# First attention of a two-attention kernel: score products made twice with full 128-row operands instead of once with transposed weights

## The chip, the cores and the metric

The kernel runs on one core of one Trainium2 chip. The metric is the device time of a launch in microseconds (us). Every engine of the core (TensorE, VectorE, ScalarE, GpSimd) runs its own instruction stream; in the profile they are PE, DVE, ACT and POOL, and SyncE, which only issues DMAs, is SP. Semaphores order the streams. TensorE reads SBUF and writes PSUM (8 banks of 128 x 512 floats); VectorE and ScalarE read and write both; GpSimd is used on SBUF alone here.

## What is computed

The reference is a chain of six blocks on x of shape (8, 512, 128): gated feed-forward, attention, gated feed-forward, expert feed-forward, a second kind of attention, expert feed-forward. The change is in the first attention alone (16 heads of 8 dimensions, 8 sequences of 512 tokens, a band of at most 60 tokens to either side):

```python
q = (x @ Wq + bq).reshape(B, S, H, hd).transpose(0, 2, 1, 3)
k = (x @ Wk + bk).reshape(B, S, H, hd).transpose(0, 2, 1, 3)
v = (x @ Wv + bv).reshape(B, S, H, hd).transpose(0, 2, 1, 3)
scores = jnp.einsum('bhqd,bhkd->bhqk', q, k) * inv_sqrt
band = jnp.abs(idx[:, None] - idx[None, :]) <= half
scores = jnp.where(band[None, None], scores, -1e+30)
attn = jax.nn.softmax(scores, axis=-1)
out = jnp.einsum('bhqk,bhkd->bhqd', attn, v)
out = jnp.einsum('bhqd,hdk->bhqk', out, W_o)
return out.transpose(0, 2, 1, 3).reshape(B, S, D) @ Wfc + bfc
```

## The kernel before

The kernel is a row of phases with a barrier between them: a start (P), a feed-forward (F0a), the first attention (A0), and then F0b, F1a, A1, F1b. In A0 (`attn0`, lines 956 to 1374) the 8 sequences are 8 chunks, one iteration each of a loop that each engine runs in its own code; the order on an engine is the written order, and the counting semaphores named below tie the engines together.

A chunk has 4 query tiles of 128 tokens. Because of the band a tile needs only a window of 256 keys (192 at both ends of the sequence). A unit `n` (16 in a chunk) is one query tile `t = n // 4` and four heads. To keep float precision in a cheap product, q and k are split in a rounded part and a rest (`fp32r` is the rounded type), so a head has 24 rows: q-high, q-high, q-low against k-high, k-low, k-high. Head rows are padded to 32, so four heads fill 128 partitions.

Per unit before:
- PE `scores` (L1254): four products, one per head, each with 24 rows in its own quarter of the array, queries on the output's partitions.
- DVE (L1203, `tensor_tensor_reduce`): one instruction per head adds the mask and takes the maximum, `M` goes to SBUF and the maximum to `nmax`.
- ACT (L1088): one Exp per head with the maximum as its bias.
- PE `turn` (L1266): 8 transposes of the weights, so that keys are on the partitions.
- ACT (L1011, first key block) and DVE (L1013, second key block), `copy_turned`: PSUM to `PT` in SBUF (`PT` lies over `dn1`, so its name in the trace is dn).
- PE `outputs` (L1279), for two units at once: values against weights, 16 products.

At the end of a chunk PE projects q, k and v of the next (`project`, L1298 and L1304), DVE adds the biases and builds the split rows (`rows_vector`, L1158 to L1179), and then PE turns Q and K (L1314), ACT copies Q (L1071) and DVE copies K (L1188) before the next scores can start. GpSimd only adds a bias to the values (L1040) and takes a reciprocal root for a layer norm (L155). The layer norm of an older chunk (L130 to L177) and the output of the last chunk (L673 to L704) run between the units.

The phase ends with `turn_out`, divide, `turn_back`, `project_out` of the last chunk and two layer norms, one after the other.

## Time and profile before

| | |
|---|---|
| median of 3 runs | 3268.33 us (3264.53 to 3269.55) |
| the profiled execution's own time | 3267.73 us |
| its span, first to last instruction | 3265.8 us |
| PE busy | 2641.5 us, 81% |
| DVE busy | 2432.7 us, 74% |
| ACT busy | 2312.6 us, 71% |
| POOL busy | 1636.1 us, 50% |
| mean granted TensorE clock | 0.849 |

Busy time is an average over all phases. What A0 is worth is read from its own stretch: its first instruction is POOL's at 426.93 us and the next phase's first work is at 943.92 us. "Granted clock" is the share of TensorE's full speed that it was given. A matmul's end is modelled, so a matmul of 0.39 us can be followed by the next one after 0.23 us: durations of PE are read together with the distance between starts.

### The profile page before, as it was taken

To read this page: it belongs to the slowest core of one execution; us is meant where nothing else is said; L and a number is where in the kernel's file an instruction comes from. 1 tells how busy PE (TensorE), PEld (TensorE's weight loads), DVE (VectorE), ACT (ScalarE), POOL (GpSimd) and SP (SyncE) were. 2 spreads that over 40 slices of the span, in tenths; PEclk is the share of its full clock that TensorE was granted. 3 is DMA by queue.
4 is the path that set the end of the run, shared out by engine and by line. 5 is a ranking of instruction groups with operands and counts; after the bars stand their busy time and mean duration, and the time that the engine had idled before them with its cause. 6 is when DMAs were issued, how large, how long until landed. Compare 5 with 4: busy or idle time off the path is not lost. (4 is left out here: it accounts for less than half of the span.)

```text
span 3265.8 us, 44956 instructions
## 1 busy us (share of the span) xinstructions
PE 2641.5 (81%) x13816; PEld 1818.6 (56%) x13818; DVE 2432.7 (74%) x4559; ACT 2312.6 (71%) x2789; POOL 1636.1 (50%) x1225
## 2 busy tenths in 40 slices
PE   4999958888859999399996587777777877549998
PEld 3877746666648777287774232232332322248887
DVE  5677757777756777688886787877878878378887
ACT  2555547676735555377772999999999999647776
POOL 2676620000026666454443666766767576444444
PEclk9999979898979999699997667676766676679999
DMA  3111100000001111211110000000000000021111
GB/s 111 52 52 39 39 1 2 0 0 0 0 28 52 52 39 39 79 52 40 52 39 0 0 1 1 1 1 1 1 1 1 1 1 1 0 92 52 52 39 51
DMA packets 13576, 86.60 MB, mean 27 GB/s; under 512 B 2176, under 2 KB 4224, under 8 KB 4224
## 3 DMA queue, kind: packets, MB, share of 16 engines
q1 hardware_dynamic: 13440, 84.96, 7.0%
q8 instruction: 64, 1.05, 0.1%
q14 instruction: 72, 0.59, 0.1%
HBM read 82.33 MB, written 2.62 MB: 26 GB/s over the span
## 5 line engine op out<-in xcount | busy, mean ns | idle before, releaser
L1648 POOL TENSOR_TENSOR A_Y<-A_Y,A_U 128x2048 f32<-128x2048 f32 x86 | 390.0, 4556 | 225.4 <-ACT A_U L1691 225.4
L1724 DVE TENSOR_SCALAR A_U<-ps 128x1024 f32<-128x1024 f32 x256 | 309.3, 1218 | 123.2 <-POOL A_Y L1648 59.3
L1730 DVE SCALAR_TENSOR_TENSOR A_U<-ps,A_U 128x1024 f32<-128x1024 f32 x256 | 311.3, 1216 | 55.6 <-PE ps L1860 55.6
L1860 PE MATMUL ps<-A_QT,A_KT 9*128 9x512 f32 x512 | 182.2, 707 | 194.2 <-DVE A_U L1730 160.9
L477 POOL TENSOR_TENSOR F0b_h<-F0b_h,dn 128x512 f32<-128x512 f32 x128 | 212.4, 1663 | 123.5 <-DVE F0b_h L408 123.3
L477 POOL TENSOR_TENSOR F0a_h<-F0a_h,dn 128x512 f32<-128x512 f32 x128 | 212.5, 1664 | 116.3 <-DVE F0a_h L408 116.1
L1860 PEld LDWEIGHTS ps<-A_QT,A_KT 9*128 9x128 f32 x512 | 66.3, 255 | 331.6 <-DVE A_U L1730 241.3
L1648 POOL TENSOR_TENSOR dn<-dn,A_U 128x2048 f32<-128x2048 f32 x42 | 190.3, 4551 | 112.1 <-ACT A_U L1691 112.1
L1691 ACT ACTIVATE A_U<-A_U 128x2048 f32<-128x2048 f32 (+1 forms) x96 | 236.5, 2464 | 0.0
L1832 PE MATMUL ps<-A_Y,A_VA 128*32 128x512 f32 x688 | 227.5, 795 | 5.8 <-DVE A_OT L1630 3.0
L1088 ACT ACTIVATE A_M<-A_M,A_nmax 128x192 f32<-128x192 f32 (+1 forms) x512 | 203.8, 471 | 34.0 <-DVE A_nmax L1203 32.3
L445 DVE SCALAR_TENSOR_TENSOR F1b_h<-ps,F1b_cwb 128x512 f32<-128x512 f32 x256 | 175.8, 688 | 49.5 <-PE ps L253 32.9
L359 ACT ACTIVATE F1a_h<-F1a_h 128x512 f32<-128x512 f32 x256 | 158.0, 624 | 76.5 <-DVE F1a_h L445 75.2
L513 POOL TENSOR_TENSOR gated<-half_neg 128x1 f32<-128x1 f32 x128 | 29.2, 228 | 363.6 <-ACT F1a_h L359 185.2
L330 ACT ACTIVATE F0b_h<-ps 128x512 f32<-128x512 f32 x160 | 95.7, 598 | 161.9 <-PE ps L253 161.9
L330 ACT ACTIVATE F0a_h<-ps 128x512 f32<-128x512 f32 x160 | 95.7, 598 | 154.8 <-PE ps L253 154.8
L1203 DVE CUSTOM_DVE_ANT_0 A_M<-ps,A_mask 128x192 f32<-128x192 f32 (+1 forms) x512 | 169.3, 387 | 48.2 <-PE ps L1254 47.9
L1849 PE MATMUL ps<-A_QT,A_KT 28*128 28x512 f32 x512 | 167.9, 673 | 44.2 <-DVE A_U L1724 40.6
L1040 POOL TENSOR_TENSOR A_VA<-A_v_new,bv 128x384 f32<-128x384 f32 (+1 forms) x16 | 13.6, 867 | 379.3 <-PE ps L1279 366.3
L359 ACT ACTIVATE F1b_h<-F1b_h 128x512 f32<-128x512 f32 x256 | 160.9, 629 | 59.2 <-DVE F1b_h L445 54.6
L1690 ACT ACTIVATE A_Y<-A_U 128x2048 f32<-128x2048 f32 (+1 forms) x64 | 159.3, 2490 | 50.2 <-DVE A_U L1730 50.0
L445 DVE SCALAR_TENSOR_TENSOR F1a_h<-ps,F1a_cwb 128x512 f32<-128x512 f32 x256 | 172.4, 683 | 29.5 <-PE ps L253 20.2
(365 smaller groups left out, 8350.9 us busy)
## 6 DMA issues: line engine op xcount, KB each, us to landing
dn<-weight_rows SPq DMA_DIRECT2D x32, 1024.0 KB, 4.7
F1a_cwb<-weight_rows SPq DMA_DIRECT2D x16, 1024.0 KB, 4.6
F1b_cwb<-weight_rows SPq DMA_DIRECT2D x16, 1024.0 KB, 4.7
dn<-in_down SPq DMA_DIRECT2D x2, 2048.0 KB, 12.3
stage<-in_up SPq DMA_DIRECT2D x1, 2560.0 KB, 9.1
X<-in_x SPq DMA_DIRECT2D x1, 2048.0 KB, 8.2
F1a_h<-in_up SPq DMA_DIRECT2D x1, 2048.0 KB, 7.7
F1b_h<-in_up SPq DMA_DIRECT2D x1, 2048.0 KB, 7.8
```

What stands on the lines that cost most here:

```text
L330: eng.activation(h[:, j % ring, :], ps[:, (j * G) % 4, :], ACT.Silu).then_inc(s["pre_done"], 1)
L359: eng.activation(z, z, ACT.Square).then_inc(s["sq_done"], 1)
L445: eng.scalar_tensor_tensor(out=h[:, j % ring, :], in0=ps[:, j % 4, :], scalar=0.0, in1=cwb[:, j // HB, :], op0=ALU.max, op1=ALU.mult).then ...
L477: eng.tensor_tensor(z, z, cwb[:, r // HB, :], ALU.mult).then_inc(s["weighed"], 1)
L1088: last = eng.activation(m, m, ACT.Exp, scale=-1.0, bias=nmax[:, n % MR, b, r:r + 1])
L1203: last = eng.tensor_tensor_reduce(M[:, n % MR, b, r, w0:w1], ps[:, 2 * (n % 2) + b, r * WIN + w0:r * WIN + w1], mask[:, w0:w1], -1.0, 3e38 ...
L1648: eng.tensor_tensor(flat(y_slot(m, h)), flat(y_slot(m, h)), flat(Um[:, h % UR]), ALU.add).then_inc(s["t_ready"], 1)
L1691: eng.activation(u, u, ACT.Sqrt).then_inc(s["s_ready"], 2 if joined else 1)
L1724: eng.tensor_scalar(u_step(n), d_pair(n), 0.0, None, ALU.max).then_inc(s["dp_vector"], 1)
L1730: eng.scalar_tensor_tensor(out=u, in0=g_pair(), scalar=CLAMP, in1=u, op0=ALU.min, op1=ALU.mult).then_inc(s["u_ready"], 1)
L1832: last = eng.matmul(ps[j:j + 32, OUT, :], VA[:, v0:v0 + 32], y_slot(m, h)[:, kt, :], start=(kt == 0), stop=(kt == TPC - 1))
L1860: last = eng.matmul(ps[:, 4 + b, :], KT[r:r + 9, pair, kt * P:(kt + 1) * P], QT[r:r + 9, pair, :], start=True, stop=True)
```

## The change

`attn0` is written anew; nothing else changes but the list of semaphores. A unit is now a group of four heads `g = n // 4` and a tile `t = n % 4`. Its steps, with the lines of the changed kernel:

- `scores` (L1335): two products per unit. `QT` (one tile of queries, four heads in 128 partitions) stands in the array; the moving operand `KZ` is a copy of the turned keys in which all but one head's rows are zero, two heads in one product of 512 (or 384) columns. The scores are used only for their maxima.
- GpSimd `spread` (L1044) makes the four `KZ` copies of a group: `KT` times a column `own` of ones and zeros.
- DVE `maxima` (L1265): the same reduction as before, written back to PSUM in place; the negated maximum goes as a 25th row into `QA`, against a row of ones in `KA`.
- `turn` (L1319): K, Q, and, once its maxima are there, Q again, four transposes for each; ACT takes them from one bank with `take_turned` (L1107) and the second Q with `take_shifted` (L1113), which writes each head into its own zero-padded copy `QZ` (four instructions of 32 partitions).
- `shifted` (L1349, L1352): the mask as a bf16 product with the identity, and then the scores a second time, with keys on the partitions and the maximum already taken off.
- ACT `weights` (L1124): one Exp per two heads, PSUM to `PT` in SBUF.
- `outputs` (L1367): four products per unit, each in a quarter of the array's columns.

So the transposes of the weights and the copies behind them are gone. `shifted` runs 8 units behind `scores` (BEHIND) and `outputs` 9 (LAST). GpSimd also builds the split rows now (`rows_q`, `rows_k`) and adds two biases; projections, norms and output steps lie between the units, in one shared bank (SPARE).

```diff
-                        def scores(n):
-                            t, u = n // 4, n % 4
-                            lo, hi, w0, w1 = window(t)
-                            for r in range(2):
-                                for b in range(2):
-                                    g, j = unit_head(u, r, b)
-                                    last = eng.matmul(ps[:, 2 * (n % 2) + b, r * WIN + w0:r * WIN + w1],
-                                                      QT[32 * j:32 * j + 24, g, t * P:(t + 1) * P],
-                                                      KT[32 * j:32 * j + 24, g, lo:hi], start=True, stop=True)
-                            return last
+                        def scores(c, n, first):
+                            g, t = n // 4, n % 4
+                            lo, hi, w0, w1 = window(t)
+                            for i in range(2):
+                                h = 2 * n + i
+                                if h >= 3:
+                                    eng.wait_ge(s["m_ready"], c * HALVES + h - 2)
+                                elif not first and h < 2:
+                                    eng.wait_ge(s["m_ready"], c * HALVES + h - 1)
+                                eng.matmul(two(half_bank(h), w0, w1), QT[:, g % 2, t * P:(t + 1) * P],
+                                           KZ[:, g % 2, 2 * i:2 * i + 2, lo:hi], start=True,
+                                           stop=True).then_inc(s["sc_done"], 1)
+                        def shifted(c, u, taken=None):
...
+                            for i in range(2):
+                                if not (isinstance(n, int) and n == 0):
+                                    eng.wait_ge(s["exp_done"], 2 * n - 1 + i)
+                                eng.matmul(two(4 + i, w0, w1), ident_b[:, :],
+                                           mask_b[:, :].rearrange("p (b w) -> p b w", b=2)[:, :, w0:w1], start=True,
+                                           stop=False, skip_group_check=True)
+                                eng.matmul(two(4 + i, w0, w1), KT[:, g, m * P:(m + 1) * P],
+                                           QZ[:, g % 2, 2 * i:2 * i + 2, lo:hi], start=False, stop=True,
+                                           skip_group_check=True).then_inc(s["s2_done"], 1)
+                        def outputs(c, u):
...
+                            eng.wait_ge(s["exp_done"], 2 * n + 2)
...
+                            for j in range(4):
+                                last = eng.matmul(ps[32 * j:32 * j + 32, OUT0, lo:hi], VA[:, m, 4 * g + j, :],
+                                                  PT[:, m, j // 2, j % 2, w0:w1], start=(m == 0), stop=(m == TPC - 1),
+                                                  skip_group_check=True)
+                        def spread(number, g):
+                            eng.wait_ge(s["taken"], number + 1)
+                            gate_gpsimd(eng)
+                            for j in range(4):
+                                last = eng.tensor_scalar(KZ[:, g % 2, j, :], KT[:, g, :].bitcast(F32), own[:, j:j + 1],
+                                                         None, ALU.mult)
+                            last.then_inc(s["kz_ready"], 1)
+                        def take_shifted(number, dst):
+                            eng.wait_ge(s["qk_tr"], number + 1)
+                            for j in range(4):
+                                r = 32 * j
+                                last = eng.activation(dst[r:r + 32, j, :], ps[r:r + 32, TURN, :], ACT.Copy)
+                            last.then_inc(s["taken"], 1)
+                            # weights(c, u), for i in range(2):
+                                eng.wait_ge(s["s2_done"], 2 * n + i + 1)
...
+                                eng.activation(PT[:, m, i, :, w0:w1], two(4 + i, w0, w1),
+                                               ACT.Exp).then_inc(s["exp_done"], 1)
+                            for n in range(UNITS):                      # PE, chunk(c, p, done)
...
+                                scores(c, n, first)
+                                v = n - LAST
+                                if v >= 0:
+                                    outputs(c, v)
...
+                                if n % 4 == 0:
...
+                                    turn(number, KA, (g + 1) % 4)
+                                if n % 4 == 1:
+                                    turn(number, QA[:, p if g < 3 else 1 - p], (g + 1) % 4)
+                                if n % 4 == 2:
...
+                                        turn(number, QA[:, p], g - 1)
...
+                                u = n - BEHIND
+                                if u >= 0:
+                                    shifted(c, u)
```

TensorE's order, in the middle of a chunk before (A_M are the weights, dn the turned weights, ps the PSUM banks):

```order
L1254 MATMUL ps<-A_KT,A_QT 128x192 [waits A0_m_ready]
L1254 MATMUL ps<-A_KT,A_QT 128x192 x3
L1266 MATMUL ps<-ident,A_M 128x128 [waits A0_pb_copied,A0_pa_copied,A0_exp_done]
L1266 MATMUL ps<-ident,A_M 128x128 x7
L1279 MATMUL ps<-dn,A_VA 32x128 [waits A0_ot_copied,A0_pb_copied,A0_pa_copied]
L1279 MATMUL ps<-dn,A_VA 32x128 x15
L1254 MATMUL ps<-A_KT,A_QT 128x192 [waits A0_m_ready]
L1254 MATMUL ps<-A_KT,A_QT 128x192 x3
```

And in the changed kernel, from one unit's outputs to the next unit's:

```order
L1349 MATMUL ps<-A_mask_b,ident_b 128x512 [waits A0_exp_done]
L1352 MATMUL ps<-A_QZ,A_KT 128x512
L1349 MATMUL ps<-A_mask_b,ident_b 128x512 [waits A0_exp_done]
L1352 MATMUL ps<-A_QZ,A_KT 128x512
L168 MATMUL ps<-rw,xT_c 128x8 [waits A0_lg_copied,A0_xt_copied]
L168 MATMUL ps<-rw,xT_c 128x8 x3
L1335 MATMUL ps<-A_KZ,A_QT 128x512 [waits A0_m_ready] x2
L1367 MATMUL ps<-dn,A_VA 32x256 [waits A0_exp_done]
L1367 MATMUL ps<-dn,A_VA 32x256 x3
L1319 MATMUL ps<-ident,A_QA 128x128 [waits A0_taken,A0_m_ready]
L1319 MATMUL ps<-ident,A_QA 128x128 x3
```

The weights' transposes are gone; between the second scores (L1352) and the outputs that use their weights (L1367) only the next unit's first scores and, at some units, one piece of other work are left.

ScalarE's order in the changed kernel at the place where the shifted queries are taken (A_QZ are their padded copies):

```order
L1107 ACTIVATE A_QT<-ps 128x512 [waits A0_qk_tr]
L1124 ACTIVATE dn<-ps 128x512 [waits A0_pv_done,A0_s2_done]
L1124 ACTIVATE dn<-ps 128x512 [waits A0_pv_done,A0_s2_done]
L692 ACTIVATE xT_c<-ps 128x512 [waits A0_oT_tr]
L1113 ACTIVATE A_QZ<-ps 32x512 [waits A0_qk_tr]
L1113 ACTIVATE A_QZ<-ps 32x512 x3
L1124 ACTIVATE dn<-ps 128x512 [waits A0_pv_done,A0_s2_done]
L1124 ACTIVATE dn<-ps 128x512 [waits A0_pv_done,A0_s2_done]
```

Where ScalarE had four Exp and one copy for a unit, it now has two Exp, and the copies of the turned Q and K stand ahead of them.

GpSimd's order in the changed kernel over about half a chunk (before, a chunk gave it two additions and one L155):

```order
L513 TENSOR_TENSOR gated<-half_neg 128x1 [waits A0_taken]
L1044 TENSOR_SCALAR A_KZ<-A_KT,A_own 128x512 x4
L155 TENSOR_TENSOR rstd<-var_eps,half_neg 128x4 [waits A0_var_ready]
L1066 TENSOR_TENSOR X<-X,bfc 128x512
L513 TENSOR_TENSOR gated<-half_neg 128x1 [waits A0_taken]
L1044 TENSOR_SCALAR A_KZ<-A_KT,A_own 128x512 x4
L1051 TENSOR_TENSOR A_VA<-A_v_new,bv 128x16x8 [waits A0_pv_done,A0_v_taken]
L1051 TENSOR_TENSOR A_VA<-A_v_new,bv 128x16x8 [waits A0_pv_done]
```

The reciprocal root for the layer norm (L155) now stands behind a spread.

## Rows read from the trace of the kernel before

**Rows 1.** Windows: us, then busy us and instructions per engine, PEclk, DMA share, GB/s.

```profile
426.90:457.40 30.50, 11.87 (x52) 9.31 (x53) 11.75 (x39) 4.57 (x8) 12.55 (x10) 0.61 0.00 0
457.40:914.30 456.90, 375.27 (x4244) 299.00 (x4244) 336.61 (x1417) 322.45 (x746) 19.00 (x21) 0.91 0.00 0
914.30:943.90 29.60, 12.61 (x52) 9.77 (x52) 8.94 (x38) 3.37 (x6) 2.01 (x2) 0.57 0.00 1
672.80:730.80 58.00, 47.89 (x538) 38.35 (x538) 42.97 (x181) 40.67 (x95) 2.72 (x3) 0.91 0.00 0
```

**Rows 2.** Timeline of PE: start us, us, engine, line, operation, count, idle before and releaser.

```profile
672.85 2.00 PE L1298 MATMUL ps<-qkv_w_s,A_xa 128*128 128x256 f32 x8 [0.45 <-DVE A_nmax L1203]
...
730.91 2.00 PE L1298 MATMUL ps<-qkv_w_s,A_xa 128*128 128x256 f32 x8 [0.46 <-DVE A_nmax L1203]
```

**Rows 3.** Groups by line, one chunk (672.8 to 730.8): busy us, mean ns, idle before.

```profile
L1266 PE MATMUL ps<-ident,A_M 128*128 128x128 f32 (+1 forms) x128 | 19.1, 297 | 4.1 <-DVE dn L1013 3.8 <-ACT dn L1011 0.2
...
L1203 DVE CUSTOM_DVE_ANT_0 A_M<-ps,A_mask 128x192 f32<-128x192 f32 (+1 forms) x64 | 21.1, 387 | 5.8 <-PE ps L1254 5.8
L1013 DVE COPY dn<-ps 128x512 f32<-128x512 f32 (+1 forms) x15 | 10.3, 686 | 1.2 <-PE ps L1266 1.2
...
L1011 ACT ACTIVATE dn<-ps 128x512 f32<-128x512 f32 (+1 forms) x19 | 11.0, 590 | 10.2 <-PE ps L1266 10.2
```

**Rows 4.** Timeline of PE in the feed-forward ahead: rounded products of 512 columns.

```profile
300.56 0.39 PE L269 MATMUL ps<-F0a_hl,F0a_dn_hi 128*128 128x512 f32 x1
300.79 0.39 PE L270 MATMUL ps<-F0a_hl,F0a_dn_hi 128*128 128x512 f32 x1
```

**Rows 5.** Timeline in A0: outputs of two units; four transposes.

```profile
645.45 1.08 PE L1279 MATMUL ps<-dn,A_VA 128*32 128x128 f32 x32
...
682.97 0.60 PE L1314 MATMUL ps<-ident,A_QA 128*128 128x128 f32 x4
```

**Rows 6.** Timeline of the phase's end: a hand-over from PE to ACT to PE.

```profile
923.12 0.60 ACT L692 ACTIVATE A_oT<-ps 128x512 f32<-128x512 f32 x1 [8.21 <-PE ps L687]
923.77 1.78 PEld L697 LDWEIGHTS ps<-out_w,A_oT 128*128 128x128 f32 x8 [1.09 <-ACT A_oT L692]
```

**Rows 7.** Groups by line and form, ACT, all of the span.

```profile
L1088 ACT ACTIVATE A_M<-A_M,A_nmax 128x256 f32<-128x256 f32 x256 | 108.8, 497 | 2.0 <-DVE A_nmax L1203 0.3
...
L330 ACT ACTIVATE F0a_h<-ps 128x512 f32<-128x512 f32 x160 | 95.7, 598 | 154.8 <-PE ps L253 154.8
...
L1088 ACT ACTIVATE A_M<-A_M,A_nmax 128x192 f32<-128x192 f32 x256 | 95.0, 445 | 32.0 <-DVE A_nmax L1203 32.0
```

**Rows 8.** Timeline of ACT: two copies from PSUM in a row.

```profile
909.64 1.07 ACT L1011 ACTIVATE dn<-ps 128x512 f32<-128x512 f32 x2 [2.62 <-PE ps L1266]
```

**Rows 9.** Groups by line and form, POOL, all of the span.

```profile
L504 POOL TENSOR_TENSOR F1a_hl<-F1a_h,F1a_hl 128x512 fp32r<-128x512 f32 x64 | 87.7, 1370 | 9.2
...
L502 POOL CAST F1b_hl<-F1b_h 128x512 fp32r<-128x512 f32 x64 | 40.9, 639 | 8.4
L513 POOL TENSOR_TENSOR gated<-half_neg 128x1 f32<-128x1 f32 x128 | 29.2, 228 | 363.6 <-ACT F1a_h L359 185.2 <-ACT F1b_h L359 178.4
...
L1605 POOL TENSOR_SCALAR xn<-A_xa,mv,rstd 128x128 f32<-128x128 f32 x32 | 25.1, 795 | 1.6 <-issue 1.6
...
L1518 POOL TENSOR_SCALAR A_nrm<-A_nrm 128x128 f32<-128x128 f32 x9 | 4.9, 549 | 1.4 <-issue 1.4
...
L1516 POOL TENSOR_SCALAR A_nrm<-A_nrm 128x128 f32<-128x128 f32 x9 | 2.7, 299 | 0.0
```

**Rows 10.** Timeline of POOL: the two layer norms at the phase's end.

```profile
928.31 1.01 POOL L155 TENSOR_TENSOR rstd<-var_eps,half_neg 128x4 f32<-128x4 f32 x1 [66.52 <-DVE var_eps L135]
936.68 1.01 POOL L155 TENSOR_TENSOR rstd<-var_eps,half_neg 128x4 f32<-128x4 f32 x1 [7.37 <-DVE var_eps L135]
```

**Rows 11.** Windows inside chunks: the columns of rows 1.

```profile
655.00:658.00 3.00, 3.00 (x50) 2.34 (x50) 2.15 (x10) 2.97 (x8) 0.00 (x0) 1.00 0.00 0
...
691.00:694.00 3.00, 2.99 (x14) 2.50 (x15) 2.20 (x13) 1.77 (x6) 0.00 (x0) 0.50 0.00 0
```

More of the change, by code:

```diff
@@ new lines, in _ @@
+                        all_chunks(eng, chunk)
+                        for n in range(LAST):
+                            if n % 4 == (LAST + 3) % 4 and n < LAST - 1:
+                                copy_out(B - 1, (n - LAST + UNITS) // 4)
+                            if n == 2:
+                                take_shifted(2 + TURNED * B, QZ[:, 1])
+                            if n < BEHIND:
+                                weights(B - 1, n + UNITS - BEHIND)
+                            if n == 3:
+                                norm_scalar(eng, s, B, B - 2, nxt, SPARE)
@@ L1362, in _, with project @@
-                        chunk(0, True)
-                        with eng.Fori(1, B) as c:
-                            chunk(c, False)
+                        def project(part):
+                            for t in range(TPC):
+                                last = eng.matmul(ps[:, SPARE, t * P:(t + 1) * P], xa[:, t * P:(t + 1) * P],
+                                                  qkv_w[lay][:, part * D:(part + 1) * D], start=True, stop=True)
+                            last.then_inc(s["pj_done"], 1)
@@ new lines, in turn @@
+                        def turn(number, src, g):
+                            eng.wait_ge(s["taken"], number)
+                            for t in range(TPC):
+                                last = eng.transpose(
+                                    ps[:, TURN, t * P:(t + 1) * P],
+                                    src[:, t, 4 * g:4 * g + 4, :].rearrange("p h r -> p (h r)").bitcast(F32),
+                                    ident[:, :])
+                            last.then_inc(s["qk_tr"], 1)
@@ new lines, in _ @@
+                        all_chunks(eng, chunk)
+                        for n in range(LAST):
+                            outputs(B - 1, n + UNITS - LAST)
+                            if n == 2:
+                                eng.wait_ge(s["m_ready"], B * HALVES)
+                                turn(2 + TURNED * B, QA[:, 1], 3)
+                            if n < BEHIND:
+                                shifted(B - 1, n + UNITS - BEHIND, 2 + TURNED * B + 1 if n == 4 else None)
+                            if n == 3:
+                                eng.wait_ge(s["x_added"], B - 1)
+                                norm_turn_tensor(eng, s, B, SPARE)
+                            if n == 5:
+                                norm_logits_tensor(eng, s, B, nxt, SPARE)
```

526 lines of the change are left out of this document (271 added, 255 removed).

## The prediction, made before the changed kernel ran

> **What bounds the kernel now.** I read the windows first, to cut out the one phase that changes: from its first instruction to the next phase's first work it takes 517.0 us (30.5 until the first scores, 456.9 of chunks, 29.6 behind the last outputs) [rows 1]. All else stays as it is. The timeline of the projections gives the period of a steady chunk: 730.91 - 672.85 = 58.06 us [rows 2]. In that period no engine is full: PE 47.9, DVE 43.0, ACT 40.7, POOL 2.7 us of 58 [rows 1]. The groups of lines say why: each engine waits a little for each other. ACT's copies of turned weights wait 10.2 us for PE, DVE's reductions wait 5.8 us for PE, the transposes 4.1 us for DVE's and ACT's copies [rows 3]. So a chunk is a loop through four hands, and what counts is the length of the loop in the new order, not the sum of work. Off it lies the row that the change aims at: 128 transposes (19.1 us of PE) and the copies behind them (10.3 us of DVE, 11.0 us of ACT) [rows 3].
>
> **The new loop, a unit at a time.** TensorE's order after the change puts `outputs` of a unit one step behind its `shifted`, and `shifted` of the next unit behind that. Only the next unit's `scores` stand between. So the loop is: shifted, two Exps, outputs, perhaps a turn, shifted. Prices, all at full clock:
> - A product of 512 columns starts 0.23 us after the one ahead and lasts 0.39 [rows 4]. `shifted` is two pairs (mask, product), 0.46 us each; the first pair's data are there at 0.62, the second's at 1.08. Two matmuls of this kind are not in the trace with these operands: the mask one is bf16; I give it the same 0.23.
> - Exp from PSUM over 512 columns is not in the trace. Silu from PSUM takes 0.598 [rows 7]; Exp from SBUF with a bias column 0.497 at 256 columns and 0.445 at 192 [rows 7], so 0.81 ns a column and 0.70 at 512. Ends 0.60 and 0.70; I take 0.60, whose source is PSUM as here. Two in a row take 1.07, so the second ends 0.48 behind the first [rows 8]. The hand-over from ACT to PE took 0.05 us (923.12 + 0.60 to 923.77) [rows 6], from PE to ACT I take 0.03.
> - Exp 1 from 0.65, Exp 2 ends at 1.73, `outputs` starts at 1.78. It is 4 float products of 256 columns side by side; before, 16 of 128 columns took 1.08 for two units [rows 5], so 0.43 of issue and 0.11 to start after a stall.
> - Interior unit: 2.3 us. A unit with 384 columns: 1.9 us by the same steps (0.17 a product, Exp 0.49).
> - Three of four units add a turn: 4 transposes last 0.60 [rows 5], less the 0.16 by which a matmul's end outlasts the next one's start [rows 4], about 0.43: 1.3 us a group of four units.
> - `take_shifted`: four copies stand ahead of Exp 1. In the trace only copies of 64 or 128 partitions exist, and they cost the same 0.59 [rows 3]. Ends: 0.6 for all four if cost went with partitions, 1.9 if not (0.48 each). I take 1.9, which delays Exp 1 from 0.65 to 2.1: +1.5 us a group. The other takes and the copy of outputs are nearly beside shifted: +0.4 a group.
>
> A group: 2 x 2.3 + 2 x 1.9 + 1.3 + 1.5 + 0.4 = 11.6 us, four of them 46.4.
>
> **What comes on top in a chunk.** Between `shifted` and `outputs` PE is idle some 0.4 us behind the next scores (1.9 us where ACT takes the shifted queries). Other work put there costs what exceeds it. A projection of 128 columns is half of 2.00 us [rows 2], and there are 4 of about 1 us (q, k, v, out) and the router; those at units 6 and 14 lie in the long gap, the three at 1, 5 and 7 show 0.6 each, six sets of transposes 0.1 each: +2.2 with rounding. Waits that TensorE's queue handles cost it about 0.1 a unit, an estimate: +1.6. ACT's own extra copies: +0.5. Clock: A0's chunks ran at 0.91 [rows 1], with 1.00 where PE was busy nearly throughout and 0.50 after looser stretches [rows 11]. The new loop has PE idle 1.5 us once a group. I count one unit in sixteen at half clock, where the loop's PE part of 1.0 us doubles: +1.0.
>
> **GpSimd, the unknown.** A chunk gives it 16 `tensor_scalar` over 512 columns with a per-partition factor. Not in the trace. Nearest: two operations with two column factors on 128 columns, 0.795; one compare with a constant 0.549; multiply and add with constants 0.299; a cast of 512 columns 0.639 [rows 9]. Lower end: like the cast, 0.64. Upper end: L1605's excess over 0.19 counted per element, 4.7 ns, so 2.6 us. I take 1.4, half of that slope because here is one operation, not two. Then four take 5.6 us and GpSimd's chunk is 22.4 + two row builds of 2 x 0.64 + 1.37 [rows 9] + bias, values, root and six gates of 0.23 [rows 9], some 35 us: not full. What it does on the path: the norm's root (1.01 [rows 10]) is behind the spread after unit 0. VectorE's norm step behind `maxima(1)` waits for it, queued behind it are `maxima(2)`, and PE's scores of unit 3 wait for those. The spread starts 1.15 us behind unit 0's second scores (turned keys copied at 0.8, gate with its wait 0.33). Root done at 1.15 + 5.6 + 1.05 = 7.8 us in the chunk, the norm step to 9.0, first half of `maxima(2)` at 9.7; outputs at that place could start at 8.5: +1.4.
>
> The GpSimd row of a cast agrees with a rule that speaks for the lower end: the Trainium skill (GPSIMD Engine Reference, section 4.1) has one-input work at roughly line rate. By it the spread costs nothing on the path, a chunk is 1.4 us shorter and the time about 3230. The 0.549 row at a quarter of the columns disagrees with it, so I don't follow it.
>
> DVE's reductions now write PSUM. Not in the trace; ends 0.35 (as now, starts 0.35 apart) and 0.69 (a 512-column copy [rows 3]): 1.4 or 2.8 us a unit, below the 3.3 us of a unit, so hidden either way.
>
> **Sum.** Chunk: 46.4 + 2.2 + 1.6 + 0.5 + 1.0 + 1.4 = 53.1 us (58.1 before). The first 8 units have no second scores; they go at GpSimd's pace (turn, take, gate, spread: 7.7 us a group) and with the first projection take 17. The last 8 units are drained without new scores: 24. Until the first scores: the split rows go through GpSimd, but the projection of q no longer waits for the mask: 29 instead of 30.5. Behind the last outputs one of the two norms (936.68 - 928.31 = 8.4 us [rows 10]) is now inside the drain: 29.6 - 8.4 = 21. In all 29 + 17 + 7.5 x 53.1 + 24 + 21 = 489.3, against 517.0: -27.7. From the profiled execution's own 3267.7 us that is 3240.0, and that execution lies 0.6 us under the median of the runs: 3240. What is saved per chunk is partly spent on the drain, which before was two units.
>
> **Rivals.**
> 1. *GpSimd sets the pace, slower.* At 2.6 us for a spread's instruction GpSimd has 41.6 + 13 = 54 us a chunk, the root comes 4.8 us later, and the k rows are late for the turn at unit 12: 10 us instead of 1.4, chunk 60.7, in all about 552: 3303. It decides from about 2.05 us an instruction, where the chunk is 56.8 and 91 + 7.5 x 56.8 = 517. For it: L1605; against: the cast and L1516, which are near one element a nanosecond.
> 2. *The ring is longer than its parts.* Clock 0.91 as before means one unit in six at half, +3 us a chunk; or Exp at 0.70 with 0.1 more spacing, +3. Chunk 55 to 56: 3255 to 3262. For it: in A0 the engines never came near their sums; against: fewer hands in the loop.
> 3. *All hides.* Spread at 0.64 and the queue's 1.6 us under the drains: chunk 49.5 to 50: 3213 to 3217. For it: the cast row. A rule of the Trainium skill bears on the clock half of this: TensorE: Matmul & The Clock Gate, Part 4, says transposes do not count as TensorE being busy. By it 48 transposes of weights, q and k instead of 160 would lift the 0.91, chunk 52.1, 3233. Here the clock in a stretch full of PE work of the old mix was 1.00 [rows 11], so it gets no weight of its own.
> 4. *No change.* Chunk 56.0 to 57.4, the gain eaten: 3262 to 3275.
>
> **Chances.** Forecast (3223 to 3257) 0.52; rival 3 and below 0.14; rival 2 0.13; rival 4 0.05; rival 1 and anything slower 0.16. A change under 0.2% (6.5 us) can't be told from none with this kernel. Faster by more 0.78 (forecast, rival 3, nearly all of rival 2), within 0.05, slower 0.17. Range 3210 to 3284: below lie some 0.07, above about 0.11 (the spread's price over 2.2). The forecast's own range is 3223 to 3257.
>
> **What would show it.** In the new profile a chunk's period between two L1335 of the same unit should be 53 us; ACT's Exp (L1124) 0.60 and its wait mostly for PE; L1044 about 1.4 us, POOL 60 to 65% busy in the phase; PE's outputs (L1367) waiting for ACT; four L1113 in 1.9 us with PE idle beside them; clock in the phase at 0.95 or more. The forecast is wrong if L1044 is over 2 us, if PE waits for POOL (kz_ready) or for DVE's maxima at more than one unit a chunk, or if the clock stays at half for whole groups.

## The result, and the profile after

| | before | after |
|---|---|---|
| median | 3268.3 us (3264.5 to 3269.6) | 3253.3 us (3252.7 to 3256.0) |
| profiled execution, its own time | 3267.7 us | 3256.0 us |
| its span | 3265.8 us | 3254.2 us |
| the first attention, first instruction to the next phase's first work | 517.0 us | 508.2 us |
| PE / DVE / ACT / POOL busy | 2641 / 2433 / 2313 / 1636 | 2631 / 2335 / 2261 / 1906 |

The ratio is 0.996, 95% interval 0.9948 to 0.9971: faster, clear of the noise, by 15 us between the medians (13.4 between the means), where 28 were forecast. The time itself lies inside the forecast's own 3223 to 3257, but the gain is about half of what was forecast. Of the 11.6 us between the two spans 8.8 lie in the changed phase. Ahead of it 0.8 us are lost, and behind it 3.6 us are won, where nothing was changed; the text comes back to that under what stays open.

The windows of the changed kernel's phase (stretch, its length, busy time and instructions of each engine, granted clock, DMA) answer to [rows 1]: until the first scores, the first eight units (unit 8's scores start at 481.72), seven and a half chunks, the drain, what lies behind it, and one steady chunk.

```profile
427.70:457.30 29.60, 6.98 (x27) 5.56 (x27) 5.07 (x21) 3.37 (x6) 22.69 (x20) 0.50 0.00 0
457.30:481.70 24.40, 16.99 (x72) 14.57 (x73) 15.89 (x78) 6.94 (x12) 15.98 (x16) 0.61 0.00 1
481.70:891.10 409.40, 334.82 (x2441) 211.73 (x2469) 231.08 (x1130) 250.49 (x480) 261.99 (x257) 0.95 0.00 1
891.10:915.10 24.00, 15.43 (x128) 7.27 (x132) 4.75 (x23) 14.60 (x29) 1.04 (x1) 1.00 0.00 1
915.10:935.90 20.80, 9.49 (x48) 6.96 (x40) 5.61 (x23) 2.28 (x4) 1.01 (x1) 0.62 0.00 1
677.00:731.50 54.50, 44.43 (x333) 28.41 (x337) 32.64 (x160) 33.81 (x66) 34.76 (x34) 0.97 0.00 0
```

The forecast had 29, 17, 398.3, 24 and 21 for the first five. Three of them came out within 0.6 us. The first eight units took 7.4 us more, the chunks 11.1 us more.

The period of a steady chunk, which [rows 2] gave as 58.06 before, is read from ACT's copy of the values, once a chunk (start, length, engine, line, tiles, shapes, and in brackets the idle time before it and what ended it):

```profile
680.78 0.60 ACT L1102 ACTIVATE A_v_new<-ps 128x512 f32<-128x512 f32 x1 [0.20 <-PE ps L1311]
735.25 0.60 ACT L1102 ACTIVATE A_v_new<-ps 128x512 f32<-128x512 f32 x1 [0.23 <-PE ps L1311]
```

735.25 - 680.78 = 54.5 us (forecast 53.1). Below, "period" is always the mean over the last four distances of this copy; here they are 54.6, 54.5, 54.6, 54.5. The two chunks ahead of them took 56.1 and 57.2.

The groups of that steady chunk (line, engine, what, count, busy, mean ns, idle before and who ended it) answer to [rows 3, 5, 7, 8]:

```profile
L1044 POOL TENSOR_SCALAR A_KZ<-A_KT,A_own 128x512 fp32r<-128x512 f32 x16 | 24.8, 1564 | 0.7 <-issue 0.7
L1265 DVE CUSTOM_DVE_ANT_0 ps<-ps,A_mask 128x256 f32<-128x256 f32 x32 | 12.6, 454 | 2.7 <-PE ps L1335 2.7
L1113 ACT ACTIVATE A_QZ<-ps 32x512 fp32r<-32x512 f32 x16 | 9.4, 588 | 5.2 <-PE ps L1319 5.1
L1124 ACT ACTIVATE dn<-ps 128x512 f32<-128x512 f32 x16 | 8.7, 596 | 0.1
L1335 PE MATMUL ps<-A_KZ,A_QT 128*128 128x384 f32 x16 | 5.1, 387 | 4.0 <-DVE A_QA L1265 4.0
L1367 PE MATMUL ps<-dn,A_VA 128*32 128x256 f32 x64 | 5.6, 421 | 5.0 <-ACT dn L1124 5.0
L141 DVE TENSOR_SCALAR xn<-X,mv,rstd 128x128 f32 x4 | 2.1, 572 | 3.4 <-POOL rstd L155 3.4
```

The transposes of the weights and both copies behind them are gone, and the Exp costs 0.60 as forecast. What TensorE waits for now are two things: ACT's weights (5.0 us) and, in a single unit of the chunk, DVE's maxima (4.0 us). The timeline of that unit in another chunk, whose unit 0 began its scores at 619.89 and 620.07, shows the second wait from its root to its end:

```profile
621.27 0.60 ACT L1130 ACTIVATE A_OT<-ps 128x512 f32<-128x512 f32 x1 [0.65 <-PE ps L1367]
621.83 0.60 ACT L1107 ACTIVATE A_KT<-ps 128x512 fp32r<-128x512 f32 x1
...
622.87 6.18 POOL L1044 TENSOR_SCALAR A_KZ<-A_KT,A_own 128x512 fp32r<-128x512 f32 x4 [0.17 <-issue]
623.29 0.29 DVE L135 TENSOR_SCALAR var_eps<-mv 128x4 f32<-128x4 f32 x1
...
627.82 2.38 ACT L1113 ACTIVATE A_QZ<-ps 32x512 fp32r<-32x512 f32 x4 [1.03 <-PE ps L1319]
...
628.53 0.33 PE L1335 MATMUL ps<-A_KZ,A_QT 128*128 128x384 f32 x1
629.02 1.04 POOL L155 TENSOR_TENSOR rstd<-var_eps,half_neg 128x4 f32<-128x4 f32 x1
630.03 1.26 POOL L1066 TENSOR_TENSOR X<-X,bfc 128x512 f32 x1
630.09 2.05 DVE L141 TENSOR_SCALAR xn<-X,mv,rstd 128x128 f32 x4 [4.91 <-POOL rstd L155]
630.23 1.08 ACT L1124 ACTIVATE dn<-ps 128x512 f32<-128x512 f32 x2
632.98 0.48 PE L1335 MATMUL ps<-A_KZ,A_QT 128*128 128x384 f32 x1 [4.12 <-DVE A_QA L1265]
633.39 1.08 PE L1367 MATMUL ps<-dn,A_VA 128*32 128x256 f32 x8
634.45 0.77 PE L1352 MATMUL ps<-A_QZ,A_KT 128*128 128x384 f32 x1
```

ACT copies the turned keys (L1107) behind the outputs' copy (L1130) and has them at 622.43, so the spread starts at 622.87. The variance is there at 623.6, but GpSimd has just begun that spread and takes the root at 629.02. DVE stands 4.9 us in front of its norm step, behind it the maxima stand, and TensorE 4.1 us in front of the second half of unit 3's scores. When it goes on, `outputs` takes 1.08 us for what takes 0.64 elsewhere: the granted clock was 1.00 in 628.0 to 633.0 and 0.57 in 633.0 to 637.0, at 0.50 until 636.6 (0.50 is the lower of its two levels, 1.2 GHz; 1.00 is 2.4 GHz). It is the same in the next three chunks: the clock is at 0.50 right behind the wait and nowhere else in the chunk. So the wait is paid a second time, in clock.

The first wait, for ACT's weights, is longest at the units that follow the four copies. In this chunk that is at units 7, 11 and 15; at unit 3 the wait for the maxima lies over it:

```profile
647.79 0.42 PE L1367 MATMUL ps<-dn,A_VA 128*32 128x256 f32 x4 [1.42 <-ACT dn L1124]
...
660.72 0.64 PE L1367 MATMUL ps<-dn,A_VA 128*32 128x256 f32 x8 [1.89 <-ACT dn L1124]
...
673.12 0.42 PE L1367 MATMUL ps<-dn,A_VA 128*32 128x256 f32 x4 [1.44 <-ACT dn L1124]
```

### The profile page after: what moved, and what is told of

Read it like the earlier page. It is cut to its first block and busy times, and to the rows that moved or that the text cites. A ratio compares the mean times of both kernels' runs of the same rounds, so it can differ in the third digit from the quotient of the medians.

```text
span 3254.2 us, 42283 instructions
## 1 busy us (share of the span) xinstructions
PE 2631.1 (81%) x12174; PEld 1754.5 (54%) x12208; DVE 2334.9 (72%) x4338; ACT 2260.8 (69%) x2559; POOL 1905.7 (59%) x1486
## 5 line engine op out<-in xcount | busy, mean ns | idle before, releaser
L513 POOL TENSOR_TENSOR gated<-half_neg 128x1 f32<-128x1 f32 x179 | 37.6, 210 | 508.0 <-ACT F1a_h L359 183.0
L1265 DVE CUSTOM_DVE_ANT_0 ps<-ps,A_mask 128x256 f32<-128x256 f32 (+1 forms) x512 | 184.6, 422 | 88.8 <-PE ps L1335 83.5
L1044 POOL TENSOR_SCALAR A_KZ<-A_KT,A_own 128x512 fp32r<-128x512 f32 x132 | 204.2, 1564 | 5.6 <-issue 5.6
L408 DVE TENSOR_TENSOR F0b_h<-F0b_h,ps 128x512 f32<-128x512 f32 x160 | 109.8, 686 | 103.2 <-ACT F0b_h L330 102.6
```

Of the source, the lines that this page charges most:

```text
L1044: last = eng.tensor_scalar(KZ[:, g % 2, j, :], KT[:, g, :].bitcast(F32), own[:, j:j + 1], None, ALU.mult)
L1265: last = eng.tensor_tensor_reduce(part, part, mask[:, w0:w1], -1.0, 3e38, ALU.add, ALU.min, QA[:, p, t, 4 * g + 2 * i + b, 3 * HD:3 * HD + ...
```

## The experiments

All twelve are edits of the changed kernel. Times are medians of 4 to 6 runs. The changed kernel itself has 3253.3 us and a period of 54.5. "Clock" is the granted clock of the stretch 500 to 840, which lies in the chunks in all of them (0.95 in the changed kernel).

| experiment | time, us | ratio to before, 95% interval | period | clock |
|---|---|---|---|---|
| e1 root ahead of the spread | 3230.4 | 0.987 to 0.991 | 53.0 | 0.96 |
| e2 bias addition later | 3252.8 | 0.995 to 0.998 | 54.4 | 0.94 |
| e3 shifted queries copied behind the Exps | 3227.7 | 0.987 to 0.991 | 51.2 | 0.96 |
| e4 outputs one unit later | 3230.2 | 0.988 to 0.991 | 52.2 | 0.94 |
| e5 = e1 + e3 | 3199.1 | 0.978 to 0.981 | 48.1 | 1.00 |
| e6 a fifth instruction a spread | 3276.7 | 1.002 to 1.005 | 58.1 | 0.92 |
| e7 = e1 + e6 | 3239.6 | 0.991 to 0.994 | 53.0 | 0.97 |
| e8 = e1 + e3 + e4 | 3199.9 | 0.979 to 0.982 | 49.5 | 0.98 |
| e9 = e5 + 60 satisfied waits on PE | 3199.1 | 0.978 to 0.981 | 48.0 | 1.00 |
| e10 = e5 + turn ahead of outputs | 3192.5 | 0.976 to 0.980 | 47.2 | 1.00 |
| e11 = e5 + copies in two pairs | 3204.3 | 0.980 to 0.983 | 47.9 | 1.00 |
| e12 = e10 without the mask product | 3193.6 | 0.975 to 0.980 | 47.9 | 0.96 |

**e1: GpSimd takes the root first.**

```diff
-                            spread(turned, 1)
                             norm_gpsimd(eng, s, c)
+                            spread(turned, 1)
```

> GpSimd takes the norm's reciprocal root before it spreads the turned keys, not after. My theory for the miss: the root behind the spread stops DVE for 4.9 us, DVE's maxima stop PE's scores of unit 3 for 4.1 us, and as nothing in this loop can lend time, the whole 4 us is lost in each of 8 chunks (in the first chunk 7). Expected: DVE's wait for the root falls under 1.5 us, the steady period of a chunk from 54.5 to about 50.5 us, the time to about 3220. Rival: the stall only moves. The root can only be taken when the statistics of unit 0 are there, the spread then ends 3 to 4 us later, and PE waits for GpSimd's keys at unit 4: period 53.5 or more, time 3247 or more.

3230.4 us, 23 us less; period 53.0, not 50.5. The timeline of the same units:

```profile
610.59 1.04 POOL L155 TENSOR_TENSOR rstd<-var_eps,half_neg 128x4 f32<-128x4 f32 x1 [6.77 <-DVE var_eps L135]
611.96 6.22 POOL L1044 TENSOR_SCALAR A_KZ<-A_KT,A_own 128x512 fp32r<-128x512 f32 x4 [0.17 <-issue]
612.09 1.59 DVE L141 TENSOR_SCALAR xn<-X,mv,rstd 128x128 f32 x4
...
615.57 0.51 PE L1335 MATMUL ps<-A_KZ,A_QT 128*128 128x384 f32 x2
618.42 0.64 PE L1367 MATMUL ps<-dn,A_VA 128*32 128x256 f32 x8 [2.33 <-ACT dn L1124]
```

The wait at unit 3's scores is gone. But right behind these scores TensorE now waits 2.33 us at `outputs`, which it did not in the changed kernel: there ACT had done its four copies and two Exps (627.82 to 631.3 in the timeline above) while TensorE stood. So the two waits overlap, and each alone is worth less than its length: over four chunks the 4.1 us a chunk for the maxima are gone, and TensorE's wait for ACT's weights grew from 5.9 to 8.2 us a chunk. No wait for GpSimd's keys came in its place: the rival failed. The clock took a part, too. The one steady chunk that kept it at 1.00 (562 to 613) took 51.1 us, those at 0.97 took 52.6.

**e2: the addition of bfc goes behind the next spread.**

```diff
-                            x_c = tiles_of(c)
-                            eng.tensor_tensor(x_c, x_c, bfc..., ALU.add)
                             spread(turned + 3, 2)
+                            x_c = tiles_of(c)
+                            eng.tensor_tensor(x_c, x_c, bfc..., ALU.add)
```

> Only GpSimd's addition of bfc (1.26 us), which stands right behind the root, is moved behind the next group's spread. Theory: the norm step on DVE (four instructions, 2.05 us together, 1.11 before the change) is slow because GpSimd's two-operand addition runs beside it. Expected: those four back at 1.1 us, PE's wait at unit 3 down by 0.9, period 54.5 to 53.6, time about 3246. Rival: they are slow for another reason (they stand behind reductions into PSUM): 2.05 stays, time 3253 within 3 us.

```profile
627.43 1.11 DVE L141 TENSOR_SCALAR xn<-X,mv,rstd 128x128 f32 x4 [4.91 <-POOL rstd L155]
629.38 0.44 PE L1335 MATMUL ps<-A_KZ,A_QT 128*128 128x384 f32 x1 [3.17 <-DVE A_QA L1265]
```

The mechanism is right to the digit: four instructions in 1.11 us instead of 2.05, TensorE's wait 3.17 instead of 4.12. But the time is the same (3252.8) and the mean period 0.1 us shorter, not 0.9. Two chunks in a row show why, by their windows:

```profile
678.70:732.30 53.60, 44.46 (x338) 28.13 (x337) 31.03 (x157) 33.82 (x65) 34.62 (x35) 0.97 0.00 0
732.30:787.50 55.20, 46.08 (x337) 29.31 (x337) 30.29 (x152) 34.09 (x66) 34.80 (x35) 0.94 0.00 1
```

At the clock of the changed kernel (0.97) a chunk takes 53.6 us, as forecast. Every second chunk has a further stretch at 0.50 (766.5 to 769.9 in this one) and takes 55.2. So contention and gain are both shown at equal clock, and the clock took the gain away again. Why it fell a second time with a shorter stall the runs don't show.

**e3: `take_shifted` behind `weights`.**

```diff
-                                if n % 4 == 2:
-                                    ... take_shifted(number, QZ[:, (g + 3) % 2])
                                 u = n - BEHIND
                                 ... weights(c, u)
+                                if n % 4 == 2:
+                                    ... take_shifted(number, QZ[:, (g + 3) % 2])
```

> On ACT the four copies of the shifted queries (2.38 us a group) stand behind the two Exps of their unit, not ahead of them. They are needed two units later. Theory: ahead of the Exps they lengthen the loop shifted, Exp, outputs by their whole length less what PE has to do beside them; behind the Exps some 1.3 us of them lies beside outputs and the next shifted, so a group loses 1.0 to 1.3 us less. Expected: PE's wait for ACT at that unit gone, at the next unit 0.7 to 1.0; period 54.5 to about 50, time about 3220. Rival: the loop is bound by ACT's sum (33.8 us a chunk and the hand-overs), the copies cost the same wherever they stand: period 54 or more, time 3248 or more.

3227.7 us, period 51.2 (-3.3). Nearer the theory than the rival, though under its 4 to 5: behind the copies TensorE now waits for ACT 0.74 us at the next unit (711.28) and up to 0.94 elsewhere, as expected. Over four chunks its wait for ACT's weights fell from 5.9 to 2.4 us a chunk. Unit 3's stall stands nearly in full (4.1 and 3.3 us in turn).

**e4: LAST 10 instead of 9**, and the output steps of the last chunk at units 9 to 15 instead of 8 to 14.

```diff
-            BEHIND, LAST = 8, 9
+            BEHIND, LAST = 8, 10
...
-                            values(c, done, 2)
-                            values(c, done, 3)
                             spread(turned + 6, 3)
+                            values(c, done, 2)
+                            values(c, done, 3)
```

> outputs of a unit run one unit later (LAST 10 instead of 9), the output steps of the last chunk one unit later with them, and GpSimd adds the last two value biases behind the spread of the fourth group. Everything else stays. Theory: the loop is shifted, two Exps, outputs of the same unit, shifted; with outputs a unit later PE has scores, outputs and a turn to do beside the Exps, its wait for ACT's weights (6 to 10 us a chunk) goes, and it is bound by its own 44.6 us and the norm stall of 4. Expected: period 49 to 50 us, time 3213 to 3222. Rival: the waits at outputs are only where a general lag shows (TensorE's queue, DVE's maxima); they turn up at the scores: period 53 or more, time 3243 or more.

3230.2 us; the distances of ACT's copy of the values alternate: 56.2, 47.7, 57.4, 47.7. Two windows, each around unit 3 of a chunk, show what differs:

```profile
673.00:679.00 6.00, 4.99 (x39) 2.69 (x37) 4.87 (x20) 4.86 (x10) 2.00 (x2) 1.00 0.00 0
...
727.00:733.00 6.00, 5.03 (x27) 2.77 (x27) 3.48 (x20) 2.01 (x4) 0.00 (x0) 0.50 0.00 0
```

At the first unit 3 TensorE waited 0.97 us and kept its clock (39 matmuls in 6 us). At the second it waited 4.58 us and came back at 0.50, with 27 matmuls in 6 us. But the first chunk had paid already: at 668.20, ahead of the copy of the values, TensorE had waited 1.79 us for the maxima, and its clock was 0.50 in 668.7 to 672.0. Measured from unit 0's scores to the next chunk's, the chunks took 52.6, 51.3, 53.5 and 51.6 us, so most of the alternation lies in where the copy stands. The theory's 49 to 50 holds for neither kind: TensorE still waited 3.7 us a chunk for DVE's maxima and 2.6 for ACT's weights.

**e5: e1 and e3 together.**

> GpSimd's root ahead of the spread, and ACT's copies of the shifted queries behind the Exps: the two edits that gave 23 and 26 us alone. Theory: they hide one another. While DVE holds PE's scores of unit 3, ACT works off its four copies and two Exps of unit 2, so each edit alone leaves a part of the other wait standing. Together they should give more than the sum of the two: period below 49.4 us (54.5 less 1.9 less 3.2), some 48, time 3193 to 3203. Rival: they are worth what they are worth alone or less, because what is left is TensorE's own work and queue: period 49.5 to 50.5, time 3205 to 3213.

```profile
700.94 0.60 ACT L1102 ACTIVATE A_v_new<-ps 128x512 f32<-128x512 f32 x1 [0.23 <-PE ps L1311]
749.22 0.60 ACT L1102 ACTIVATE A_v_new<-ps 128x512 f32<-128x512 f32 x1 [0.19 <-PE ps L1311]
```

3199.1 us. Alone the edits gave 22.9 and 25.7 us, together 54.2; the period went down by 1.5, 3.3 and 6.4. So the two waits did hide one another, as expected, and the clock is 1.00. TensorE's waits over four chunks (604.8 to 797.1; total, times, longest) are what is left:

```profile
PE ps L1367 <- ACT dn L1124: 13.6, 22, 1.6
PE ps L1335 <- POOL A_KZ L1044: 3.1, 2, 1.6
```

That is 3.4 us a chunk for ACT's weights and 0.8 for GpSimd's keys. The longest of the first kind stand behind the four copies, now at units 0, 4 and 12 (0.6 to 0.75, 1.6 in every second chunk, and 0.9 us).

**e6 and e7: a spread one instruction longer**, with the root behind it (e6) and ahead of it (e7).

```diff
+                            eng.tensor_scalar(idle[:, :], KT[:, g, 0:376].bitcast(F32), own[:, 0:1], None, ALU.mult)
                             for j in range(4):
```

> GpSimd does a fifth tensor_scalar of 376 columns (about 1.15 us) ahead of the four of each spread, into a tile that nobody reads. Order of the root as in the changed kernel, behind the spread. Theory: only the root behind the first spread is on the path, so a chunk grows by 1.15 us (a little more where the longer stall costs clock) and the first two groups of the phase by as much each: period 55.7 to 56.2, time 3263 to 3269. Rival: GpSimd paces every group; then a chunk grows by 4.6 us, time about 3290. Other rival: the stall has cover and nothing changes, 3253.

> The same fifth instruction, but with the root ahead of the spread. Theory: with the root ahead the spread has slack of several us against the scores of the next group, so 1.15 us more shows only in the first two groups of the phase (2.3 us): period 52.7 as without it, time 3230 to 3234. Rival: the spread is on the path in every group all the same: 1.15 us or more a group, time 3260 or more.

e6 is 23 us slower than the changed kernel, and slower than the kernel before. Its waits over 620 to 730 (two chunks; total, times, longest):

```profile
PEld ps L1337 <- DVE A_QA L1267: 11.4, 2, 5.7
DVE xn L141 <- POOL rstd L155: 10.9, 2, 6.1
```

The stall grew by 1.2 us, as it should (4.5 to 5.7), but the chunk by 3.6. The rest fits the clock: a steady chunk had 0.97 before and has 0.91 now (689.6 to 747.7). Against full clock 1.6 us of a chunk were missing, and now 5.2 are. The difference of 3.6 us is an upper bound, since a low clock costs nothing where TensorE waits; 2.4 are needed. With the root ahead (e7) the period is that of e1, 53.0, so the spread itself is hidden; the first two spreads, which are not, grew by 1.2 us each. The median is 9 us above e1, more than the 0 to 4 expected; the profiled executions stand 2.8 us apart (3235.7 and 3232.9), so where the rest comes from is not shown.

**e8: all three edits.**

> Root ahead of the spread, copies of the shifted queries behind the Exps, outputs a unit later. Theory: with all three waits gone PE is left with its own 44.5 us of work and the gaps of its queue, at full clock: period 46 to 47 us, time 3180 to 3192. Rival: with the first two edits nothing is left for the third, which only moves the output steps: period and time as with two edits, within 4 us of it.

3199.9 us: the rival's time, but not its period, which is 1.4 us longer (49.5) at a clock of 0.98. The later outputs did hide the 3.4 us a chunk for ACT's weights that e5 has left. Others came in their place (603.4 to 801.3, a chunk): 1.9 us for ACT's copy of the output, 1.7 at the turn for GpSimd's rows of k, 1.0 for its keys and 0.9 for the maxima. The time is equal because the stretch from the last copy of the values to the next phase is 4.3 us shorter than in e5 (79.1 against 83.4).

**e9: 60 more waits on TensorE, all satisfied** (`eng.wait_ge(step, n0 + 5)` ahead of `outputs`, `turn` and each half of `shifted`).

> The kernel with root ahead and copies behind (3199 us, period 47.9), and on TensorE one more semaphore wait, satisfied since the phase began, ahead of every outputs, every turn and each half of shifted: 60 waits a chunk. Theory for what the chunk costs beyond my sum without root and copies (45.7 against 47.9): every wait that TensorE's queue handles costs it some 0.05 us beside the work, and I had counted 1.6 us a chunk in all. Expected: 60 x 0.05 = 3 us a chunk, a part of it hidden in waits, period 49.5 to 51, time 3212 to 3224. Rival: a satisfied wait costs nothing, the gaps of 0.25 to 0.4 us ahead of these groups come from what stands in the array (tiles of 32 columns, a new kind of matmul); time 3199 within 4.

3199.1 us, exactly as without them, period 48.0: a satisfied wait on TensorE costs nothing here. The theory is dead, and with it the reason for my term of 0.1 us a unit for the queue.

**e10: turn ahead of outputs.**

```diff
                                 scores(c, n, first)
-                                ... outputs(c, n - LAST)
                                 ... turn(number, ...)
+                                ... outputs(c, n - LAST)
```

> Root ahead, copies behind, and on TensorE the turn of a unit stands ahead of outputs, not behind. Theory: the loop of a unit is shifted, Exps, outputs, shifted, and what stands behind outputs lies on it (I counted 1.3 us a group for three turns), what stands ahead lies in PE's wait for the Exps. So up to 0.43 us comes back in each of 12 units a chunk, less where PE has no wait: period 47.9 to 44.5 to 46, time 3172 to 3188. Rival: with those two edits the loop is no longer what binds but PE's own work and queue, and the order of the groups is worth nothing: period 47.5 or more, 3195 or more.

3192.5 us, the fastest. Period 47.2, between theory (44.5 to 46) and rival (47.5). TensorE's waits over four chunks (601.3 to 789.9) say what stands against it:

```profile
PE ps L1319 <- POOLq L1037: 4.5, 4, 1.1
PE ps L1367 <- ACT dn L1124: 3.5, 9, 0.9
PE ps L1335 <- POOL A_KZ L1044: 3.1, 2, 1.6
```

Of the 3.4 us a chunk for ACT's weights in e5 2.5 went. But at unit 12 the turn now waits 1.1 us for GpSimd's rows of k (POOLq is GpSimd's sequencer, and L1037 the end of `rows_k`), which it did not in e5. The period fell by 0.9 us.

**e11: the four copies in two pairs**, behind the Exps of two units.

> Root ahead, copies behind, and of the four copies of the shifted queries two stand behind the Exps of this unit and two behind those of the next. Theory: four in a row still hold the next unit's Exps by some 1.6 us (PE's wait at its outputs), two in a row fit between two Exps: 1 us a group comes back, 4 a chunk, less 0.3 where PE's turn now waits for the second pair: period 44.5 to 46, time 3170 to 3185. Rival: what ACT lags in one unit it makes up in the next anyway, period 47 or more, 3193 or more.

3204.3 us, 5 us slower than e5, period 47.9: the rival. The chunks are no longer than in e5; the stretch from the last copy of the values to the next phase is (88.2 us at clock 0.83, against 83.4 at 0.88). TensorE's weight loads now wait 6.1 us in 640 to 740 for the second pair, at the turn.

**e12: e10 without the mask product.** The mask is left out of the second scores.

> The fastest version so far (root ahead, copies behind, turn ahead of outputs; 3192.5 us, period 47.1), and the mask product is left out of the second scores, so keys outside the band get a weight. Theory: of 47.1 us some 44 are now TensorE's own starts and gaps, so the mask's 32 products (0.23 apart at 512 columns, 0.17 at 384) give back nearly all of their 6.4 us and some of the 0.3 us gaps ahead of them: period 40 to 42, time 3146 to 3162. Rival: the loop shifted, Exp, outputs still binds; the mask lies on it only with its first half, 0.2 us a unit: period 43.5 to 44.5, time 3168 to 3176. Other rival: GpSimd (35 us) or ACT (36) or DVE (32.5) with their waits bind; period over 45.5.

3193.6 us: nothing came back for 32 matmuls fewer in a chunk. Theory and first rival failed. The second rival's sign, a period over 45.5, is there (47.9). Stretch 500 to 840 of e10, and of e12:

```profile
500.00:840.00 340.00, 311.64 (x2420) 195.06 (x2420) 219.76 (x1092) 242.65 (x473) 245.29 (x240) 1.00 0.00 1
```

```profile
500.00:840.00 340.00, 291.36 (x2173) 188.78 (x2172) 219.67 (x1092) 240.38 (x469) 245.41 (x240) 0.96 0.00 1
```

PE is busy 20 us less, and DVE and GpSimd get through the same number of instructions (1092 and 240). TensorE's waits over four chunks (600.3 to 792.0):

```profile
PE ps L1319 <- POOLq L1037: 8.8, 4, 2.3
PE ps L1335 <- POOL A_KZ L1044: 4.8, 5, 1.8
PE ps L1364 <- ACT dn L1124: 4.5, 13, 0.6
```

For GpSimd, its rows of k and its keys, TensorE waits 3.4 us a chunk where it was 1.9 in e10. So with the mask's products gone GpSimd is what TensorE waits for most, which speaks for the second rival. The clock is no longer whole, either. The two steady chunks that kept it took 45.1 and 46.0 us (46.4 to 47.3 in e10), the four that lost it for some us 46.8 to 49.0. So of 6.4 us only 1 to 2 were on the path at full clock, and a clock of 0.96 took them back. Between 500 and 830 the clock fell five times, each time within 1.3 us of the end of a wait of 1.8 to 2.3 us for GpSimd; four other such waits were not followed by a fall. The longest wait in e10 is 1.6 us, and its clock did not fall there. Whether the waits or the fewer matmuls brought it down, the runs don't separate.

## Why the prediction was right and wrong

Right were the direction, the loop (shifted, two Exps, outputs) and three of its five stretches [rows 1]; the Exp (0.60); DVE's reductions into PSUM, a little longer (0.42 us in the mean of both shapes for 0.39 [rows 3]) and hidden; and that GpSimd's spread would be neither 0.64 nor 2.6 us but near 1.4: it is 1.56. GpSimd is busy 64% in a steady chunk (34.8 of 54.5), as forecast. The rule cited for the lower end (the Trainium skill, GPSIMD Engine Reference, section 4.1) does not hold for this instruction: 1564 ns for 512 columns against 0.61 for a cast of as many.

In its size the forecast was off by 18.9 us in the phase (489.3 against 508.2), less 2.8 us that the rest of the program gave back. By its own steps:

1. **The first 8 units: 17 us forecast, 24.4 measured.** I let them run at the pace of turn, copy, gate and spread, 7.7 us a group. The root behind the spread stopped the first group, too. GpSimd had the keys of the second group ready at 466.35, but TensorE stood 7.0 us at unit 3 for the maxima, and unit 4 started at 471.47: 5.1 us of the 7.4. With the root ahead (e1) the first eight units took 22.1 us, not 17, because the root, and with it the spread, then waits for the first statistics (4.1 us). Turn, copy, gate and spread took more than 7.7 us, too: 9.1 in each group (457.26 to 466.35, and 471.47 to 480.57). The stretch ran at clock 0.61, where I took full clock.
2. **The root's place: 1.4 us a chunk forecast, a stall of 4.1 measured.** Who waits for whom was right, and so was the moment at which TensorE could have gone on (8.8 us behind unit 0's second scores, forecast 8.5). Wrong was the moment of the maxima: 9.7 forecast, 12.9 measured (620.07 to 632.98). The spread starts 2.8 us behind unit 0's second scores, not 1.15: I had the turned keys copied at 0.8, but the turn stands behind `outputs` on TensorE and the copy behind the outputs' copy on ACT, so they are there at 2.4 (622.43). The spread takes 6.2 us for my 5.6, and the norm step 2.05 for about 1.2, since GpSimd's addition runs beside it (e2). Taking the root away gave 1.5 us a chunk alone (e1) and 3.1 where the copies no longer hid it (51.2 to 48.1, e3 to e5), a part of it clock.
3. **The four copies: 1.5 us a group, 6.0 a chunk.** They cost 2.38 us together, not 1.9: instructions on 32 partitions followed each other at 0.60 us and did not overlap as the two of [rows 8] do. What TensorE waits behind them is 1.42, 1.89 and 1.44 us in three groups, near the 1.5 forecast. In the fourth it lies under the stall of step 2, so the chunk pays some 4.75 us and not 6.0. Behind the Exps the copies gave 3.3 us a chunk (4.9 with the root ahead), and in e5 some 2.4 us of waits behind them are left.
4. **The rest of the chunk: 45.7 us forecast (53.1 less 1.4 and 6.0), 48.1 measured in e5.** The clock term was not even needed there (1.00), so the gap is 3.4 us. Of these, 2.4 are the waits that the copies still cause (step 3), and 0.8 is a wait for GpSimd's keys, which the sum had at nothing. That nearly closes the gap, but only if the 1.6 us for TensorE's queue stand, and e9 took their reason away. So about 1.8 us of the chunk have no shown cause. The turns, 1.3 us a group in the sum, gave back 0.9 us a chunk when they stood ahead of `outputs` (e10).
5. **Clock.** Forecast 1 us a chunk, from one unit in sixteen at half. The steady chunk had 0.97, so 1.6 us, but not spread: it comes behind the stall. That fits a stall that costs more than its length (e6: 1.2 us longer, 3.6 us more).

A steady chunk took 54.5 us for 53.1. The stall is 2.7 us more than its term and the copies 1.3 less, which makes the difference. The other terms (clock, queue, the rest) missed as well, and that they cancel is luck.

So the failed steps are 1 and 2, and the root is behind both. Its term was 1.4 us a chunk and nothing in the first eight units; the runs showed a stall of 4.1 us in each steady chunk and of 7.0 in the first. The spread in front of the root started 1.65 us later than forecast and took 0.6 us longer, and the norm step behind it took 0.85 us longer. Of the rivals the second ("the ring is longer than its parts", chunk 55 to 56, 3255 to 3262) came nearest; its reasons, clock 0.91 or a slower Exp, were not the ones. (In the fourth rival a chunk of 57.4 us gives 3272 us, not 3275.) As to the rule cited there (the Trainium skill, TensorE: Matmul & The Clock Gate, Part 4): the clock of a steady chunk did rise with fewer transposes, from 0.91 [rows 1] to 0.97. But with the same transposes it was 0.91 in e6 and 1.00 in e5, so the stalls weigh at least as much here, and no run separates the two.

Open: before the phase and behind it nothing was changed, and yet the stretch from the first work of the next phase to the end is 2318.3 us where it was 2321.9. It was 2317 to 2320 in all twelve experiments. The difference lies in phase F1a, which takes 412.4 us from its first work to its last where it took 416.0, at a granted clock of 0.94 in both. There is one profile of the kernel before, and other executions of it spread over 15 us (3256 to 3271), so the cause stays open.

## What to carry to other kernels

Where a short instruction that another engine waits for is put behind a long one on an idle engine, follow the wait to its end: who stands behind the waiting engine, whether the last one is the engine that sets the pace, at what moment the long one can start at all, and in which cycle of the pipeline there is nothing to hide it yet. Two waits that lie over each other must be taken away together: alone they gave 23 and 26 us here, together 54. And work taken from TensorE is not time gained before its new waits and its granted clock have been read: e12 had 6 us a chunk less to do and was no faster, with 1.5 us a chunk more of waiting for GpSimd and a clock of 0.96.

## What the runs showed that I had not expected

- After a wait of 4 us TensorE came back at a reduced clock (0.57 over 633 to 637), after 4.6 us in e4 at 0.50 for 6 us, and after 1.79 us in e4 at 0.50 for 3.3 us; after 0.97 us it kept its clock (e4). The four kernels with a clock of 1.00 in their chunks (e5, e9, e10, e11) have no wait over 1.6 us there. In e12, with fewer matmuls and longer waits for GpSimd, the clock went from 1.00 to 0.96.
- `tensor_scalar` on GpSimd with one factor per partition: 1.56 us for 512 columns, 3.1 ns a column, where a cast of 512 takes 0.61.
- The norm step's four small DVE instructions took 2.05 us beside GpSimd's `tensor_tensor`, 1.59 beside its `tensor_scalar` (e1), 1.11 beside nothing (e2).
- An ACT copy from PSUM on 32 partitions costs what it costs on 128: 0.588 against 0.598 us.
- A satisfied semaphore wait on TensorE costs nothing that can be measured: 60 a chunk, 3199.1 and 3199.1 us (e9).
